# Eight-head attention: who sends the rows of the maximum, and what SyncE waits for before it replicates keys

## The reference, cut to what matters

```python
h = ((g - mu) * jax.lax.rsqrt(var + EPS)).reshape(B, C, T) * gn_w[:, None] + gn_b[:, None]
qkv = (jnp.einsum('oc,bct->bot', qkv_w, h) + qkv_b[:, None]).reshape(B * NUM_HEADS, 3 * ch, T)
q, k, v = (qkv[:, :ch], qkv[:, ch:2 * ch], qkv[:, 2 * ch:])
w = jax.nn.softmax(jnp.einsum('bct,bcs->bts', q * scale, k * scale), axis=-1)
a = jnp.einsum('bts,bcs->bct', w, v).reshape(B, C, T)
return (xr + jnp.einsum('oc,bct->bot', proj_w, a) + proj_b[:, None]).reshape(x.shape)
```

## Time and profile before

| | before |
|---|---|
| median of 3 runs | 2487.98 us (2482.21 to 2491.14) |
| the profiled execution, its own time | 2498.52 us |
| span of the profiled execution | 2496.8 us |
| PE, DVE, ACT busy | 87%, 70%, 66% |
| mean granted TensorE clock | 0.912 |
| `many_heads` (first to last exponential, L599) | 90 to 1913 us |

### The profile page before, as it was taken

The page is one execution under the profiler, slowest core; times in us unless marked ns, Lnnn a source line. Parts: engine busy times, 40 slices in busy tenths (PEclk is TensorE's granted clock), DMA queues, the critical chain, the costliest instruction groups (busy, mean ns, idle before and its releaser), DMA issues. The chain is left out here.

```text
span 2496.8 us, 32884 instructions
## 1 busy us (share of the span) xinstructions
PE 2173.1 (87%) x11778; PEld 1069.3 (43%) x11778; DVE 1743.4 (70%) x2115; ACT 1657.4 (66%) x3009; POOL 458.5 (18%) x682
## 2 busy tenths in 40 slices
PE   1888879897888988797978889888988999999999
PEld 0333323333333333233333333333332788888887
DVE  1776768685776867675857668676761777777776
ACT  0366657574666666575757667665765888888887
POOL 4102011110202020111101020201000333333331
PEclk7699999897989998888979899989995999999999
DMA  5144251505052341515050523415100111111111
GB/s 76 15 57 60 43 74 42 87 20 83 25 78 49 54 70 33 77 39 85 18 87 24 79 43 60 65 37 74 43 24 27 53 62 61 53 49 51 61 49 45
DMA packets 56101, 133.00 MB, mean 53 GB/s; under 512 B 13600, under 2 KB 24992, under 8 KB 55968
## 3 DMA queue, kind: packets, MB, share of 16 engines
q1 hardware_dynamic: 55968, 131.27, 28.7%
HBM read 53.12 MB, written 17.83 MB: 28 GB/s over the span
## 5 line engine op out<-in xcount | busy, mean ns | idle before, releaser
L485 DVE TENSOR_REDUCE h_half_nmax<-h_s_ps 128x2 f32<-128x1024 f32 x1024 | 1207.2, 1220 | 451.0 <-PE h_s_ps L666 446.7
L599 ACT ACTIVATE h_probs<-h_st_ps 128x512 f32<-128x512 f32 x2048 | 1069.1, 602 | 543.5 <-PE h_st_ps L773 527.7
L773 PE MATMUL h_st_ps<-h_qrep,h_krep 51*128 51x512 f32 x2048 | 690.3, 504 | 209.4 <-DMA h_qrep<-h_mrow 179.6
L773 PEld LDWEIGHTS h_st_ps<-h_qrep,h_krep 51*128 51x128 f32 x2048 | 294.4, 197 | 783.1 <-ACT h_probs L599 434.3
L656 PE MATMUL h_pv<-h_probs,h_vT 128*32 128x512 f32 x4096 | 591.8, 652 | 0.0
L666 PE MATMUL h_s_ps<-h_krep,h_qrep 48*128 48x512 f32 x2048 | 397.3, 448 | 74.3 <-SPq L237 30.5
L666 PEld LDWEIGHTS h_s_ps<-h_krep,h_qrep 48*128 48x128 f32 x2048 | 211.5, 203 | 185.9 <-DVE h_half_nmax L485 87.2
L1295 PE MATMUL o_s<-o_k,o_q 128*128 128x512 f32 x768 | 223.9, 428 | 8.1 <-DVE o_q L1116 5.7
L378 POOL TENSOR_SCALAR h_nparts<-h_nmax 128x16 bf16<-128x16 f32 x64 | 16.3, 255 | 1131.0 <-DVE h_nmax L492 1131.0
L1295 PE MATMUL o_pv<-o_pT,o_vT 128*128 128x512 f32 x768 | 207.3, 406 | 0.8 <-ACTq L1222 0.8
L1110 DVE TENSOR_TENSOR o_pT<-o_t,o_pT 128x512 fp32r<-128x512 f32 x256 | 164.5, 684 | 42.4 <-ACT o_pT L1247 38.9
(11 more groups left out here) (106 smaller groups left out, 1247.6 us busy)
## 6 DMA issues: line engine op xcount, KB each, us to landing
h_krep<-h_kp SPq DMA_DIRECT2D x96, 256.0 KB, 9.2
h_qrep<-h_qp SPq DMA_DIRECT2D x96, 256.0 KB, 18.1
x_res<-out_dram SPq DMA_DIRECT2D x24, 512.0 KB, 3.7
num<-av SPq DMA_DIRECT2D x128, 64.0 KB
rrep<-rden_dram SPq DMA_DIRECT2D x16, 512.0 KB
out_dram<-o_y SPq DMA_DIRECT2D x16, 512.0 KB
out_dram<-h_y SPq DMA_DIRECT2D x15, 512.0 KB, 2.7
o_x_in<-out_dram SPq DMA_DIRECT2D x15, 512.0 KB, 3.6
```

The source lines that it names most:

```text
L485: reduce = nc.vector.tensor_reduce(half_nmax[:, c, th, :, pair % MP], s_ps[slot][:, :, :], AX.X, ALU.max, negate=True)
L599: nc.scalar.activation(probs[g % 2][:, j, :], st_ps[n % COLUMN_BANKS][:, :], ACT.Exp, scale=1.0 / CH ** 0.5).then_inc(columns_done, 1)
L773: nc.tensor.matmul(st_ps[n % COLUMN_BANKS][:, :], krep[par][part, quad * 2 + m, st * P:(st + 1) * P], qrep[par][part, quad * 2 + m, th * H ...
```

## The change

ACT issues the transfer of `mrow` itself, right behind its copy, as two DMAs instead of four. `qrep` has its two halves of the queries outside the head pairs, so that the rows of one half are one piece, and the order of the parts in `nparts` follows. `mrow_ready` goes. SP has no `max_rows` left. It issues the six DMAs of the keys right behind the broadcast read of the reciprocals, waits for the reciprocals after that, and then issues those of the queries, twelve of 128 KB instead of six of 256 KB. DVE makes the reciprocals ahead of group 5 instead of 6.

```diff
-        qrep = [sb(f"qrep{i}", [P, HEADS // 2, T], F32R) for i in range(2)]
+        qrep = [sb(f"qrep{i}", [P, 2, HEADS // 2, HALF], F32R) for i in range(2)]
...
-        nparts = [sb(f"nparts{i}", [P, 2, 2, MAX_PARTS, MP // 2], BF16) for i in range(2)]
+        nparts = [sb(f"nparts{i}", [P, 2, MAX_PARTS, MP], BF16) for i in range(2)]
...
-            def replicate(par, u):
...
+            def replicate_keys(par, n):
+
+                sp.wait_ge(parts_ready, n)
+                for term, part in enumerate((0, 0, 1)):
+                    for r in range(2):
+                        to, of = r * ROWS + term * CH, slice(r * ROWS, (r + 1) * ROWS)
+                        sp.dma_start(krep[par][to:to + CH, :, :].bitcast(F32),
+                                     parts["k"][of, part, :].bitcast(F32)).then_inc(rep_dma, 16)
+
+            def replicate_queries(par, n):
+
+                sp.wait_ge(parts_ready, n)
+                for term, part in enumerate((0, 1, 0)):
+                    for r in range(2):
+                        to, of = r * ROWS + term * CH, slice(r * ROWS, (r + 1) * ROWS)
+                        for th in range(2):
+                            sp.dma_start(qrep[par][to:to + CH, th, :, :].bitcast(F32),
+                                         parts["q"][of, part, th * HALF:(th + 1) * HALF].bitcast(F32)).then_inc(rep_dma, 16)
+
+            def replicated():
+
+                sp.wait_ge(rep_dma, 16 * 6 * TERMS)
+                sp.sem_inc(rep_dma, -16 * 6 * TERMS)
                 sp.sem_inc(rep_ready, 1)
                 sp.sem_inc(parts_free, 1)
...
                         spread()
-                    max_rows(4 * u + 1, u, 0, 1)
-                    if not (last and u == 1):
-                        replicate(1 - u, u)
-                    max_rows(4 * u + 2, u, 1, 0)
...
+                    if more:
+                        replicate_keys(1 - u, 2 * u + 1)
+                    if of_image_before:
+                        spread_done()
+                    if more:
+                        replicate_queries(1 - u, 2 * u + 2)
+                        replicated()
...
-                        if s % 2 == 0 and k == 6:
+                        if s % 2 == 0 and k == 5:
...
-            def max_rows(n, bank, th):
+            def max_rows(n, bank, step, th):
 
                 act.wait_ge(columns_ready, n)
                 own.done(nc.scalar.copy(mrow[th][:, :], st_ps[bank][:, :].bitcast(BF16)[0:MAX_PARTS * MH, 0:P]))
                 act.sem_inc(columns_done, 1)
-                act.sem_inc(mrow_ready, 1)
+                par, quad = step // 2 % 2, step % 2
+                for r in range(2):
+                    act.dma_start(qrep[par][r * ROWS + KS:r * ROWS + KM, th, quad * 2:(quad + 1) * 2, :].bitcast(F32),
+                                  mrow[th][r * MAX_PARTS * MP:(r + 1) * MAX_PARTS * MP, :].bitcast(F32)).then_inc(mrow_dma, 16)
...
-                            pe.wait_ge(mrow_dma, 64 * (2 * s + k // TILES + 1))
+                            pe.wait_ge(mrow_dma, 32 * (2 * s + k // TILES + 1))
```

More of the change, by code:

```diff
@@ L201, in many_heads @@
         nparts_ready = sem("nparts_ready")
-        mrow_ready = sem("mrow_ready")
         mrow_dma = sem("mrow_dma")
@@ L257, in _ @@
             sp.wait_ge(ones, 1)
-            replicate(0, 0)
+            replicate_keys(0, 1)
+            replicate_queries(0, 2)
+            replicated()
             sp.sem_inc(parts_ready, -2)
@@ L286, in spread, with spread_done @@
                 sp.dma_start(rrep[:, :], rden_dram.rearrange("h (a t) -> h a t", a=1).to_broadcast([HEADS, CH, T])).then_inc(den_dma, 16)
+            def spread_done():
                 sp.wait_ge(load_dma, 16)
@@ L295, in body @@
                     i = 2 * pair + u
[L297 to L300, removed]
+                    of_image_before = not (first and u == 0)
+                    more = not (last and u == 1)
+                    if of_image_before:
                         sp.wait_ge(av_ready, 2 * u + 1)
@@ L304, in body @@
                         spread()
-                    max_rows(4 * u + 1, u, 0, 1)
-                    if not (last and u == 1):
-                        replicate(1 - u, u)
-                    max_rows(4 * u + 2, u, 1, 0)
+                    else:
+                        sp.sem_inc(av_ready, 1)
+                        sp.sem_inc(rden_ready, 1)
+                    if more:
+                        replicate_keys(1 - u, 2 * u + 1)
+                    if of_image_before:
+                        spread_done()
+                    if more:
+                        replicate_queries(1 - u, 2 * u + 2)
+                        replicated()
                     sp.wait_ge(y_ready, 2 * (u + 1))
@@ L325, in body @@
                     kept["gather"](sp, 0, av_dma)
-                    max_rows(4 * u + 3, u, 1, 1)
-                    if not (last and u == 1):
-                        max_rows(4 * u + 4, 1 - u, 0, 0)
                 if not last:
                     sp.sem_inc(parts_ready, -4)
-                    sp.sem_inc(mrow_ready, -8)
                 sp.sem_inc(av_ready, -4)
@@ L374, in split_max @@
                 pool.wait_ge(nmax_ready, n)
-                new = nmax[:, th * MH:(th + 1) * MH].rearrange("p (m t) -> p m t", t=MP // 2)
-                left = nrest[:, :].rearrange("p (m t) -> p m t", t=MP // 2)
-                to = nparts[th][:, :, :, :, :].rearrange("p r m a t -> p (r m) a t")
+                new = nmax[:, th * MH:(th + 1) * MH].rearrange("p (r m) -> p r m", r=2)
+                left = nrest[:, :].rearrange("p (r m) -> p r m", r=2)
+                to = nparts[th]
                 own.done(nc.gpsimd.tensor_scalar(to[:, :, 0, :], new, 1.0, None, ALU.mult))
@@ L578, in _ @@
                 evacuate(n + 1, n % COLUMN_BANKS, which, c)
-            max_rows(5, 4 % COLUMN_BANKS, 0)
+            max_rows(5, 4 % COLUMN_BANKS, 0, 0)
             act.sem_inc(columns_ready, -5)
@@ L609, in body @@
                             if k == MAX1:
-                                max_rows(n + 1, bank, 1)
+                                max_rows(n + 1, bank, s, 1)
                             elif k == MAX0:
-                                max_rows(n + 1, bank, 0)
+                                max_rows(n + 1, bank, s + 1, 0)
                             else:
@@ L648, in transpose_max @@
                 nc.tensor.transpose(st_ps[bank][:, :].bitcast(BF16)[0:MAX_PARTS * MH, 0:P],
-                                    nparts[th][:, :, :, :, :].rearrange("p r m a t -> p (r m a t)"),
+                                    nparts[th][:, :, :, :].rearrange("p r a b -> p (r a b)"),
                                     ident[:, :]).then_inc(columns_ready, 1)
@@ L665, in row_scores @@
                     rows = slice(r * ROWS, r * ROWS + KS)
-                    product = nc.tensor.matmul(s_ps[slot][:, r, :], qrep[par][rows, m, th * HALF + tile * P:th * HALF + (tile + 1) * P],
+                    product = nc.tensor.matmul(s_ps[slot][:, r, :], qrep[par][rows, th, m, tile * P:(tile + 1) * P],
                                                krep[par][rows, m, c * HALF:(c + 1) * HALF], start=True, stop=True)
@@ L773, in column_scores @@
                             nc.tensor.matmul(st_ps[n % COLUMN_BANKS][:, :], krep[par][part, quad * 2 + m, st * P:(st + 1) * P],
-                                             qrep[par][part, quad * 2 + m, th * HALF:(th + 1) * HALF],
+                                             qrep[par][part, th, quad * 2 + m, :],
                                              start=True, stop=True).then_inc(columns_ready, 1)
@@ L791, in body @@
                     return
-                pe.sem_inc(mrow_dma, -64 * 8)
+                pe.sem_inc(mrow_dma, -32 * 8)
                 pe.sem_inc(rep_ready, -2)
```

2 lines of the change are left out of this document (removed).

## The result

The changed kernel takes 2671.14 us (2669.03 to 2677.17) against 2486.59 us of the kernel before on the same chip: a ratio of 1.0746, 95% interval 1.0718 to 1.0774, 7.5% slower. I had said 2322.

The account below looks back on a forecast made before the run. No engine is full, so waits decide: PE waits for the rows of the maximum, held up by SP's order. The terms -247 + 79 = -168 us gave 2322 us, range 2275 to 2425.

Parts of the forecast that it names:

- step 1: Rows of the maximum no longer go through SP: stall A, stall B and the long clock go, 247 us at most.
- stall B: PE's wait at group 0 of the odd step, while SP waits for the replications: 5.46 us in 15 images, 82 us.
- the long clock: Granted clock staying longer at its lower level behind stall B in six images: 3.3 us each, 20 us.
- step 3: Landing of the rows of group 8 sent by ACT: 1.3 us behind the issues, with 3.5 us of cover.
- stall A: PE's wait at group 8 of the even step, with SP amid the reciprocals: 9.66 us in 15 images, 145 us.
- row A late: Rival, 30%: rows of group 8 take turns with bulk pieces, land 4 to 5.5 us late; 100 us given back, 2422.
- The slower rival: Rows of group 8 wait behind all SP's queued traffic, 12.3 us late; 2537 us; 4% with the like.
- Step 2: Two ACT issues behind each copy delay the next exponential by 1.25 us, 63 times: 79 us more.
- Step 4: SP issues keys about 12.5 us earlier at cost 0; replications taking 29.5 us hide the queries, with 15 us of cover.
- Step 5: Reciprocals at group 5: DVE's wait is 0, the spread comes about 3 us earlier, worth nothing by itself.

Follow-up runs that it names:

- e6_keys_behind_rows: Changed kernel with SP waiting, before it issues the keys, until ACT has issued the rows of group 8: 2445.35 us, ratio 0.9831 to the kernel before.
- e4_sp_rows_first: Changed kernel, but SP sends the rows with two DMAs, those of group 8 ahead of the keys, and ACT issues none: 2282.46 us, ratio 0.9161.
- e7_issues_apart: On `e1_keys_after`, ACT issues its two DMAs one behind each first exponential of the next two groups, not behind the copy: 2321.94 us, ratio 0.9339.
- e1_keys_after: Changed kernel with SP issuing the keys behind its wait for the reciprocals again, ACT still sending the rows: 2453.09 us, ratio 0.9835 to the kernel before.

## Why the prediction was wrong, point by point

**What bounds the kernel**: right. The stalls were SP's order, and with both gone and nothing put in their place the kernel takes 2282 us where the kernel before took 2495 beside it: 212 us of the 247 that step 1 had as its limit, with 26 us of waiting at group 8 left.

**Step 1, stall B** (-82, and its part of the long clock): right, -107 measured.

**Step 1 with step 3, stall A** (-145): the step that failed. Step 3 saw that the rows would fly beside the read and the keys, and then took the landing from a queue with nothing ahead of it: 1.3 us behind the issue, 3.5 us of cover. They landed 22 us behind it, and A cost 115 us more than before instead of 145 less. `e6_keys_behind_rows` and `e4_sp_rows_first` show the cause by taking it away: the keys that SP had queued just before, four of them ahead of the rows and the last two beside them, together with the read. The 1.3 us was no price of the transfer; how long the rows take to land hangs on what SP has issued ahead of them.

**The rival "row A late"** had 30% and one of the two halves of the truth. Its turns are in the trace: 48 pieces, some three at a time every 0.55 us, in 8.2 us (6.5 to 9.7 over the images), against the 48/3 x 0.56 = 9.0 it worked out. It had no place for the 12.6 us before the first piece, and so priced 100 us where 260 were due (-145 to +115). The Trainium skill (DMA: Bandwidth & Descriptors, "Queues, rings and completion order") has an engine drain 9 to 17 descriptors of one queue before it changes; in 13 of the 14 images with the stall the trace disagrees, since the pieces spread over those 8 us in nearly even steps. In the first image it agrees: there the first 24 pieces and their three completions move in one burst of 0.7 us. What the prediction made of this rule, "about 1 us late at most", has no working; by its own 0.56 us, 9 to 17 pieces of the bulk take 5.0 to 9.5 us, which is 1.5 to 6 us beyond the cover of 3.5. That three engines carry them, as the same page says of 3 partitions and 24 rows, fits the rate, and it fits the packets of q10: 3456 for 128 DMAs are 27 each, 24 pieces and three completions. No row names the engines.

**The slower rival**: "row A waits behind all the traffic that SP has queued", against which I held that it "would need one common queue for both issuers". It did not need one, and its mechanism is the one that the packets show: the first piece waits for what had been issued ahead, and the last one moves with the last of the keys. I had given it 4%. The rows were 16 us late, more than its 12.3, although ACT's queue is its own. Its time, 2537, was short of the result by the cost of the clock and by the turns on top.

**Step 2, the issues** (79 us): right in kind, 93 measured. An issue took 0.73 us and the pair delayed the loop by 1.47 us, not 1.25. The argument that nothing in the loop makes it up was right, and `e7_issues_apart` shows the other side of it: behind the first exponential there is room for it.

**The clock behind the issues** was no term at all. I took the low clock for a mark of the long stalls and said that there would be none without them. It cost 75 us here and 99 in `e1_keys_after`. With it and 93 instead of 79, the predicted 2322 would have been about 2410 even if the rows had landed in time; `e1_keys_after`, where they did, took 2453.

**Step 4**: the order of issues on SP cost nothing by itself, but the replication took some 36 us instead of 29.5 (its last packets move at about 766 us in the image shown); the cover of 15 us took that up. **Step 5**: right, no new wait of DVE.

## What to carry to other kernels

Before a small, urgent transfer is given to another engine's queue, look at what the first queue issues around that moment. The order of issue counts across queues, and here a hold of 3.4 us on the bulk in each image was worth some 225 us. An issue on a compute engine has a place where it is free and one where it costs its full time. Put it behind the instruction that the slowest engine waits for, not in front of it. And count short pauses twice, once as themselves (93 us here) and once for the clock behind them (75 us here, 99 in `e1_keys_after`).

## What the runs showed of the hardware that I had not expected

- A transfer on ACT's queue did not start for 12.6 us because SP had issued a read and four bulk copies ahead of it on its own queue; it started when about 380 of their 384 pieces had started. Issued 1.5 us ahead of the copies it started after 2.6 us, behind the read alone. Where in the chip the rows wait (where descriptors are made, or in the engines) is open.
- A pause of 1.5 us at the first exponential of one group in eight was followed by a mean granted clock of 0.77 over the next 6 us in the stretch shown, so by the lower level (1.2 GHz) for nearly half of it. With the same issues one exponential later, the groups behind them had their full speed (clock 1.00 in the stretch shown).
- Bulk copies inside the chip's SBUF took 31 to 36 us when they were issued within 1 us behind a read of 512 KB from DRAM, and 27 to 29.4 us when they were issued 4 us behind it or more.
- A DMA issue on ACT takes 0.73 us of its sequencer, but runs beside an activation that has already started. The Trainium skill (DMA: Bandwidth & Descriptors, "Issuing engines are not separate DMA queues") calls the sequencer's time "usually small relative to the DMA itself"; here a pair of issues takes 1.5 us and its last piece moves 2.4 us behind the first issue, and 64 such pairs in the wrong place cost 192 us.
